# Attention values of two key heads as stacked high and low parts: 16 products for 24 per unit, halves added by a DMA that accumulates

## The reference, cut to what matters

```python
q, k, v = split(x @ w_qkv.T + b_qkv)          # 32 query heads, 8 key/value heads of 32
q = apply_rope(q, 0); k = apply_rope(k, 0)
k = jnp.repeat(k, GROUP, axis=1); v = jnp.repeat(v, GROUP, axis=1)      # GROUP = 4
scores = jnp.einsum('bhqd,bhkd->bhqk', q, k) / math.sqrt(HEAD_DIM)
attn = jax.nn.softmax(jnp.where(causal, scores, -1e20), axis=-1)
out = jnp.einsum('bhqk,bhkd->bhqd', attn, v)                            # the products that change
```

## Time and profile before

| | |
|---|---|
| median of 3 runs | 1154.16 us (1153.38 to 1154.23) |
| the profiled execution | 1153.42 us, its span 1151.3 us |
| matmuls | 6176 |
| busy: PE, PEld, DVE, ACT, POOL | 98%, 86%, 59%, 36%, 18% of the span |
| granted TensorE clock | 0.998 of full speed |
| DMA | 98.3 MB, 26% of 16 engines' time |
| chain that ended last | PE 87%, DVE 7%, ACT 4%, DMA 1% |

### The profile page before, as it was taken

One profiled execution on the slowest core, in us unless ns is written; L12 is line 12 of the kernel. 1 busy time (PEld: TensorE's weight loads), 2 busy tenths in 40 slices (PEclk: granted clock), 3 DMA queues, 4 the chain that ended last, 5 costly groups with the idle time before them and its releaser, 6 DMA issues.

```text
span 1151.3 us, 16982 instructions
## 1 busy us (share of the span) xinstructions
PE 1132.6 (98%) x6176; PEld 992.3 (86%) x6176; DVE 684.9 (59%) x1201; ACT 409.2 (36%) x1172; POOL 202.8 (18%) x131
## 2 busy tenths in 40 slices
PE   8999999999999999999989999999999999999998
PEld 6888888999999999999889998888888888888887
DVE  5312137878887888888894234233136766666664
ACT  5312124555555555555553234111123322222221
POOL 0000124443334433334351001000000000000000
PEclk9999999999999999999999999999999999999999
DMA  8020032111111111110042115473561323332222
GB/s 287 18 66 19 10 113 73 46 46 52 58 46 46 46 54 46 46 46 36 19 169 92 57 38 165 128 217 101 158 183 43 123 110 110 111 110 96 75 69 92
DMA packets 90082, 98.29 MB, mean 85 GB/s; under 512 B 7730, under 2 KB 74162, under 8 KB 90034
## 3 DMA queue, kind: packets, MB, share of 16 engines
q1 hardware_dynamic: 89890, 97.37, 26.2%
q10 hardware_dynamic: 144, 0.26, 0.1%
HBM read 72.45 MB, written 25.17 MB: 85 GB/s over the span
## 4 chain that ended last, share of the span: by engine, by line
PE 87%; DVE 7%; ACT 4%; DMA 1%; issue 0%; POOL 0%; DVEq 0%; SPq 0%
PE psum L912 18%; PE psum L1563 15%; PE psum L1871 14%; PE psum L280 13%; PE psum L1291 8%; PE psum L1851 4%; PE psum L974 4%; PE psum L1949 4%; ACT prob L617 3%; PE psum L944 3%; PE psum L959 2%; PE psum L931 1%; PE psum L991 1%; DVE prob L838 1%; DVE smax L836 1%; DVE prob L834 1%
## 5 line engine op out<-in xcount | busy, mean ns | idle before, releaser
L912 PE MATMUL psum<-p_h,c_high_low 128*128 128x512 f32 (+1 forms) x768 | 194.3, 360 | 0.5 <-DVE qkv L867 0.5
L912 PEld LDWEIGHTS psum<-p_h,c_high_low 128*128 128x128 f32 x768 | 133.2, 188 | 14.2 <-issue 0.7
L280 PE MATMUL psum<-c_high_low,w_h 128*128 128x512 f32 x384 | 119.5, 396 | 5.7 <-ACT c_high_low L215 5.7
L1563 PE MATMUL psum<-ring,rows 128*128 128x512 f32 x528 | 123.7, 392 | 1.0 <-DVE t_plain L1265 0.8
L1563 PEld LDWEIGHTS psum<-ring,rows 128*128 128x128 f32 x528 | 98.8, 188 | 23.9 <-DVE t_plain L1265 2.3
L1291 PE MATMUL psum<-chunk,rows 128*128 128x384 f32 (+1 forms) x576 | 108.7, 343 | 1.2 <-DVE qkv L867 0.7
L912 PE MATMUL psum<-p_l,c_high_low 128*128 128x512 f32 (+1 forms) x384 | 104.2, 366 | 0.0
L1291 PEld LDWEIGHTS psum<-chunk,rows 128*128 128x128 f32 x576 | 101.8, 190 | 2.0 <-DVE qkv L867 1.0
L280 PEld LDWEIGHTS psum<-c_high_low,w_h 128*128 128x128 f32 x384 | 73.4, 191 | 22.4 <-ACT c_high_low L215 5.7
L704 POOL TENSOR_TENSOR prob<-prob,sinv 128x1024 f32<-128x1024 f32 x32 | 61.1, 1908 | 126.7 <-DVE sinv L771 126.7
L694 POOL TENSOR_TENSOR c_high_low<-ring_plain,c_high_low 128x512 fp32r<-128x512 f32 x32 | 41.4, 1293 | 235.0 <-PE psum L280 139.1
(11 more groups left out here) (172 smaller groups left out, 2225.1 us busy)
## 6 DMA issues: line engine op xcount, KB each, us to landing
ring_plain<-in_x_t SPq DMA_DIRECT2D x32, 256.0 KB, 2.6
attn_scratch<-ring_plain SPq DMA_DIRECT2D x16, 512.0 KB, 2.6
ring_plain<-attn_scratch SPq DMA_DIRECT2D x32, 256.0 KB, 4.0
raw<-x_t_scratch SPq DMA_DIRECT2D x16, 512.0 KB, 4.1
rest<-in_b_base SPq DMA_DIRECT2D x16, 512.0 KB, 4.2
out<-rest SPq DMA_DIRECT2D x15, 512.0 KB, 2.7
ring_plain<-in_wqkv_t SPq DMA_DIRECT2D x10, 512.0 KB, 6.1
a_raw<-in_lora_a SPq DMA_DIRECT2D x32, 128.0 KB, 2.1
```

What stands on the lines that cost most here:

```text
L280: mm = pe.matmul(to, stationary, moving, start=k == 0 and m == 0, stop=k == KT - 1 and last, skip_group_check=True)
L912: mm = pe.matmul(to, sx[:, kk, :], moving(w, n, kk), start=first, stop=False, skip_group_check=True)
L1563: mm = pe.matmul(self.psum[:, self.BANK_OF[i], :], w[:, cols], s, start=m == 0 and p == 0, stop=m == KT - 1 and p == 2, skip_group_check=True)
```

## The change

Values: one block `vb[:, b, q, j]` holds high part and low part side by side, each with the two head columns of the pair: 2 parts x 2 heads x 32 = 128 columns. One matmul with the high probabilities gives the high product in PSUM rows 0 to 63 and the low one in rows 64 to 127. A second matmul with the low probabilities uses only the high part, 64 columns, and accumulates into rows 0 to 63. Pairs j now have PSUM columns of their own, so one b fills both banks, and b=1 waits until b=0 has been copied out (`pv_out`). Per unit 16 matmuls stand where 24 stood. ACT copies each b out in two pieces (j = 0, 1), into `ring` slot 2 and a new tile `values_odd`. When b=1 is out, POOL issues two DMAs that add rows 64 to 127 to rows 0 to 63 in SBUF, and SP stores two halves instead of one whole. In `BESIDE` the entries from `attend` b=1 on stand one pass later. Behind step 16 the loads of `b2_up` and of the first half of chunk 1 are issued ahead of the last store. The diff, without declarations:

```diff
-    def diag(vb, b, h):
+    def diag(part, b, h):
 
-        flat = vb[h * SEQ:(h + 1) * SEQ, b, :, :, :, :].rearrange("p q j c d -> p q (j c d)")
-        return flat.rearrange("p q (m d) -> p q m d", d=HD)[:, :, h:h + 7:6, :]
+        return vb[h * SEQ:(h + 1) * SEQ, b, :, :, part, h, :]
...
+            if value and not score:
+                sp.wait_ge(s_done, 2 * UNITS)
+                fold2.load_lora(sp)
+                sp.wait_ge(fold2.row_low, fold2.STAGED)
+                fold2.load_chunk(sp, 1, 0)
             if value:
-                sp.wait_ge(pv_out, 2 * w + 2)
-                sp.dma_start(a["attn"][bass.ds(w, 1), :, :].rearrange("o p c -> (o p) c"),
-                             attn[:, :, :, :].rearrange("p k b t -> p (k b t)")).then_inc(stored, 16)
+                sp.wait_ge(pv_summed, 32 * w + 32)
+                for j in range(2):
+                    sp.dma_start(a["attn"][bass.ds(w, 1), j * SEQ:(j + 1) * SEQ, :].rearrange("o p c -> (o p) c"),
+                                 values[j][high_rows, :]).then_inc(stored, 16)
...
         def values_out(w, b):
             act.wait_ge(pv_done, 2 * w + b + 1)
             if b == 0:
-                need(act, stored, 16 * w)
-            act.activation(attn[:, :, b, :], s_ps[:, b, :].rearrange("p (k t) -> p k t", k=KT), ACT.Copy).then_inc(pv_out, 1)
+                need(act, stored, 32 * w)
+            for j in range(2):
+                to = values[j].rearrange("p (k b t) -> p k b t", k=KT, b=BPU)[:, :, b, :].rearrange("p (q g) t -> p q g t", q=QUADS)
+                cols = s_ps[:, :, j * GRP * SEQ:(j + 1) * GRP * SEQ].rearrange("p q (g t) -> p q g t", g=GRP)
+                last = act.activation(to, cols, ACT.Copy)
+            last.then_inc(pv_out, 1)
...
+        def add_low_values():
+            for j in range(2):
+                pool.dma_start(values[j][high_rows, :], values[j][low_rows, :], accum_op=ALU.add).then_inc(pv_summed, 16)
...
+            if value:
+                pool.wait_ge(pv_out, 2 * w + 2)
             if nxt:
                 split_x(u + 1, 0)
...
+            if value:
+                add_low_values()
             if score:
                 normalise(v, 0)
...
-            n = 0
-            for vv, pp in ((vb_h, pt_h), (vb_l, pt_h), (vb_h, pt_l)):
+            else:
+                pe.wait_ge(pv_out, 2 * v + 1)
+            for parts, pp in ((2, pt_h), (1, pt_l)):
...
-                        mm = pe.matmul(s_ps[:, b, q * 4 * SEQ:(q + 1) * 4 * SEQ], vv[:, b, q, j, :, :].rearrange("p c d -> p (c d)"),
-                                       pp[:, q, j, :, :].rearrange("p g t -> p (g t)"), start=n == 0, stop=pp is pt_l and j == 1, skip_group_check=True)
+                        v_at = vb[:, b, q, j, 0:parts, :, :].rearrange("p m h d -> p (m h d)")
+                        mm = pe.matmul(s_ps[0:parts * SEQ, q, j * GRP * SEQ:(j + 1) * GRP * SEQ], v_at, pp[:, q, j, :, :].rearrange("p g t -> p (g t)"),
+                                       start=parts == 2 and j == 0, stop=parts == 1 and j == 1, skip_group_check=True)
...
-                  (2, 1): [(attend, 2, 1), (transpose_qk, 1, (0, 1))], (3, 1): [(transpose_qk, 1, (2,))],
-                  (4, 0): [(scores, 1, 0)], (5, 0): [(scores, 1, 1)]}
+                  (2, 2): [(attend, 2, 1), (transpose_qk, 1, (0, 1))], (3, 2): [(transpose_qk, 1, (2,))],
+                  (4, 1): [(scores, 1, 0)], (5, 1): [(scores, 1, 1)]}
```

More of the change, by code:

```diff
@@ L465, in attention @@
     v_hl = sb("v_hl", [P, 2, QUADS, 2, 2, HD], F32R)
-    vb_h, vb_l = (sb(n, [P, BPU, QUADS, 2, 4, HD], F32R) for n in ("vb_h", "vb_l"))
+    vb = sb("vb", [P, BPU, QUADS, 2, 2, 2, HD], F32R)
+    values = ring[:, 2, :], sb("values_odd", [P, D])
     prob = sb("prob", [P, BPU, 2, KVH, SEQ])
@@ L469, in attention @@
     pt_h, pt_l = (sb(n, [P, QUADS, 2, 2, P], F32R) for n in ("pt_h", "pt_l"))
-    attn = ring[:, 2, :].rearrange("p (k b t) -> p k b t", k=KT, b=BPU)
     cos, sin = sb("cos", [P, HD // 2]), sb("sin", [P, HD // 2])
@@ L497, in attention @@
     pt_done, pt_high, pt_low = sem("pt_done"), sem("pt_high"), sem("pt_low")
-    pv_done, pv_out, stored = sem("pv_done"), sem("pv_out"), sem("attn_stored")
+    pv_done, pv_out, pv_summed, stored = sem("pv_done"), sem("pv_out"), sem("pv_summed"), sem("attn_stored")
     consts = [(b_bc[:, :], a["b_qkv"].partition_broadcast(P)), (cos[:, :], a["cos"]), (sin[:, :], a["sin"]),
@@ L576, in sync @@
         steps(sp, step)
-        sp.wait_ge(stored, 16 * UNITS)
+        sp.wait_ge(stored, 32 * UNITS)
     def high_x(act, u, half):
@@ L657, in step @@
                 act.wait_ge(v_high, v + 1)
-                act.wait_ge(vb_zero, 2)
+                act.wait_ge(vb_zero, 1)
                 need(act, pv_done, 2 * v)
@@ L661, in step @@
                     for h in range(2):
-                        last = act.activation(diag(vb_h, b, h), v_hl[b * SEQ:(b + 1) * SEQ, 0, :, :, h, :].bitcast(F32), ACT.Copy)
+                        last = act.activation(diag(0, b, h), v_hl[b * SEQ:(b + 1) * SEQ, 0, :, :, h, :].bitcast(F32), ACT.Copy)
                 last.then_inc(vb_high, 1)
@@ L734, in gpsimd @@
         pool.wait_ge(fold1.done, fold1.TILES * fold1.STEPS)
-        pool.memset(vb_h[:, :, :, :, :, :].bitcast(F32), 0.0).then_inc(vb_zero, 1)
-        pool.memset(vb_l[:, :, :, :, :, :].bitcast(F32), 0.0).then_inc(vb_zero, 1)
+        pool.memset(vb[:, :, :, :, :, :, :].bitcast(F32), 0.0).then_inc(vb_zero, 1)
         steps(pool, step)
@@ L821, in step @@
                 dve.wait_ge(v_low, v + 1)
-                dve.wait_ge(vb_zero, 2)
+                dve.wait_ge(vb_zero, 1)
                 need(dve, pv_done, 2 * v)
@@ L825, in step @@
                     for h in range(2):
-                        last = dve.tensor_copy(diag(vb_l, b, h), v_hl[b * SEQ:(b + 1) * SEQ, 1, :, :, h, :].bitcast(F32))
+                        last = dve.tensor_copy(diag(1, b, h), v_hl[b * SEQ:(b + 1) * SEQ, 1, :, :, h, :].bitcast(F32))
                 last.then_inc(vb_low, 1)
@@ L1342, in sync @@
     def sync(sp):
[L1343 to L1346, removed]
+        fold.load_chunk(sp, 1, 1)
+        for s in range(2, fold.STEPS):
             for h in range(2):
-                if s > 1:
-                    sp.wait_ge(fold.chunk_low, KT * (s - 1) + HALF * (h + 1))
+                sp.wait_ge(fold.chunk_low, KT * (s - 1) + HALF * (h + 1))
                 fold.load_chunk(sp, s, h)
```

4 lines of the change are left out of this document (2 added, 2 removed).

## The result

| | before | after |
|---|---|---|
| median of 6 runs | 1153.99 us (1153.16 to 1154.23) | 1159.22 us (1157.71 to 1160.25) |
| profiled execution, span | 1151.3 us | 1158.4 us (its own time 1160.25) |
| loop's period, `up` to `up`, mean of 14 steps | 27.27 us | 27.60 us |

The ratio is 1.0045, 95% interval 1.0035 to 1.0055: slower by a half per cent, as forecast, with 128 matmuls fewer. The 14 steps of the loop take 381.8 us before and 386.4 after, which gives 4.6 of the 5.2 us between the medians.

The account below looks back on a forecast made before the run. A loop through PE, DVE and ACT, as long as PE's own work (27.25 us), was taken as the bound. Products gain 0, the second copy costs 0.40 us a step; 14 x 0.40 = +5.6 us gives 1159.4 us, range 1150 to 1166.

Parts of the forecast that it names:

- Products and moved pass: PE, attend b=1: 0.94 us saved goes to the moved pass (0.74) and a 0.2 us wait for low probabilities; gain 0.
- Second copy: ACT: keys queue behind two copies of b=1, so they and everything behind them on ACT and DVE move 0.49 us.
- Scores +0.30 and a waiting start of +0.10: PE: scores start 0.30 us later, their waiting first matmul takes 0.10 more; together +0.40 us a step.
- From scores to `up`, 10.29: DVE's chain from scores b=0 to `up`: fixed 10.29 us, holding no instruction of the change.
- PE waits ahead of `up` by 0.9 us or so: Sign: PE waits for the low LoRA rows ahead of `up` by 0.9 us or so in each step.
- PE's busy time falls by some 15 us: Sign on PE: busy time falls by some 15 us while the span grows.
- POOL and the store: POOL's two DMA issues fit its 7.41 us idle; accumulation and store have 14 us; nothing expected on the path.
- A: Rival, ACT ahead of keys: second copy fits the 0.19 us slack, period stays 27.25, time 1153 to 1156; chance 0.17.
- B: Rival: PE alone is the bound, so the 15.0 us come out in full, 1139; chance 0.11.
- C: Rival: POOL's DMAs stretch DVE's L838 by 1.40 us a step, or accumulation and store run late; 1179; chance 0.10.
- The ends: Steps 16 and 17: the copy's 0.49 us loss set against attend's 0.47 to 0.94 gain; 0, give or take 0.5.
- DVE works without a break: DVE from `up` to low probabilities b=1: continuous work ending 339.48, which nothing in the change makes earlier.

Follow-up runs that it names:

- Run 1: Kernel before plus one more ACT copy of 512 elements a row from PSUM right ahead of the keys, nothing else: 1159.28 us, ratio 1.0049.
- run 4: Changed kernel with both copies of b=1 on DVE, behind the low probabilities, instead of on ACT: 1155.13 us, ratio 1.0010.
- run 2: Kernel before without the products of low values and high probabilities, so 16 products for 24: 1154.78 us, ratio 1.0007.
- run 3: Changed kernel with the BESIDE table of before, so no pass stands later: 1158.62 us, ratio 1.0043.
- run 5: Changed kernel without the two accumulating DMAs, the store waiting for the copies alone: 1157.79 us, ratio 1.0038.
- run 12: Kernel before with one exchange on DVE, low probabilities of b=1 ahead of the low values: 1152.28 us, ratio 0.9990.
- run 8: Kernel before, DVE reordered: LoRA copy and low LoRA rows early, low probabilities b=1 ahead of low values; 24 products: 1157.48 us, ratio 1.0033.
- run 6: Changed kernel with DVE's LoRA copy ahead of b=0's reciprocal and low LoRA rows ahead of b=1's sum: 1159.4 us, ratio 1.0049.
- run 10: Changed kernel, b=1's copies on DVE, lows and low probabilities earlier, rotation sums split between POOL (after all four products) and DVE: 1144.12 us, ratio 0.9920.

## Why the prediction was right

The time was forecast at 1159.4 us and measured at 1159.22; the path was the forecast's too. That the two agree to 0.2 us is luck: the loop lost 4.6 us where the sum has 5.6, and the rest of the 5.2 lies outside the loop, where the sum has 0 and the executions scatter by 2 us with the clock. That the change costs some 5 us, and why, isn't luck: runs 1 and 4 show it from both sides.

- *Products and moved pass, gain 0.* Right. The transposes stand at 10.56 us from `up`, 10.59 before; the wait said to be 0.2 us is 0.24. Runs 2 and 3 show each half of it by itself.
- *Second copy, +0.49 on the keys.* Right: keys 0.98 us after the first copy. From the transposes to the keys it was 0.69 and is 1.17.
- *Scores +0.30 and a waiting start of +0.10.* The scores came 0.29 later against the transposes (5.02 for 4.73), the start cost 0.09. With the 0.03 by which the transposes came earlier, that is 0.35 at DVE's mask and 0.36 at the next `up` of this step, and 0.33 in the mean of the 14 steps, where 0.40 was said; the before step that was read, 27.25 us, is 0.02 under the mean of its kind. Run 1 has it without the rest of the change, run 4 takes it away.
- *From scores to `up`, 10.29.* 10.30, and the subtraction, L838 before and L856 now, at 1.22 us.
- *PE waits ahead of `up` by 0.9 us or so.* The amount is right, the place mostly wrong. By start times PE lost 0.57 us more than before ahead of L1004 and 0.17 more ahead of `up`, together the 0.74 of the moved pass. The text didn't name the wait at L1004, where the transpose of the LoRA rows waits for DVE's copy of them. It costs nothing, since `up` waits for the same engine behind it.
- *PE's busy time falls by some 15 us.* Wrong: by 5.4 us. In runs 2 and 3 it fell by 13.0 and 11.9. The likeliest reading, which no run tested by itself, is that busy time counts a matmul to its modelled end: a group of four has 0.47 us of pitch and 0.63 of busy time, so that the first 0.16 us of a wait look busy. After has three or four short waits a step, run 2 has a long one and run 3 a long and a short one. The clock has a part too: run 5, with after's order on PE and 1.000 throughout, has 1123.9 us, 3.3 less than after. PEld's busy time fell from 992.3 to 977.8, by 14.5 us. The Trainium skill's page "Perfetto Trace Analysis" (Identifying the Most-Contended Engine) says that how close TensorE is to its limit is to be read from the busy share of weight loads (and from the share of peak work), not from that of matmuls. The profiles of before and after agree in so far as 14.5 is near the 15.0 us of products and 5.4 is not; but half of the products' loads became shorter as well (137 ns for 188), so the nearness is in part chance. The forecast should have named this measure.
- *POOL and the store.* Right. SP issued the store at 328.48, 5.3 us after the issue of the second addition, and POOL kept 5.88 us of room. The estimate by the Trainium skill's page "DMA: Bandwidth & Descriptors" (Anatomy of one DMA), 2.6 us for 256 KB, was low: 3.5 and 5.1 us here.
- *The rivals.* A needed the copy to fit into 0.19 us; it took 0.48. B fell with run 2, C with run 5.
- *The ends*, 0 give or take 0.5: not resolved. The loop gives 4.6 of 5.2 us, and the remaining 0.6 is less than what the clock behind the loop moves (2 us between executions of after). The forecast had no term for the clock.

What the prediction lacked is the third member of its own loop. It treated `up` to the low probabilities as fixed, "DVE works without a break", and didn't ask what in that stretch was dear. The 2.22 us row, which served only as a price for rival C, was the place at which the kernel could be made faster.

## What to carry to other kernels

An engine that is busy for 98% can still be paced by a loop through the others: lay one step of each engine side by side, and compare what an operand's producer leaves as slack with what the change takes away. Before taking work from an engine, see whether its place in the loop waits for something, and count what the change puts ahead of the next handoff on the other engines; one copy of 0.49 us cost 0.33 us a step, and 0.94 us of matmuls gave nothing. And where several pieces tie, take them together: against the kernel before, the low probabilities first gave 1.5 us (run 12) and the two orders of DVE cost 3.8 (run 8), in the changed kernel the lows first gave nothing (run 6), and all of them with the 16 products, the copies on DVE and the split gave 0.8% (run 10).

## What the hardware showed that I had not expected

- A DVE operation on 128x640 with two operands in SBUF took 0.82 us alone. Beside an operation of POOL that had started before it, it ended 0.68 us behind POOL's end, however long that was: it took 2.22 us beside the first rotation sum in before (POOL ends at 337.33, DVE at 338.01), 1.53 us in run 6 (336.15 and 336.83), 1.31 us in run 10 (334.26 and 334.94). POOL's first rotation sum started while DVE's product before it was still running, and took 2.11 us in before where the one in run 10, beside the low probabilities, took 1.60. The low probabilities, with one operand in PSUM, took 1.21 to 1.23 us in all places. The Trainium skill's page "SBUF — State Buffer" (SBUF: two separate sides) says that of a DVE operation with two SBUF inputs and a GpSimd operation that reads SBUF the one that starts first holds the shared port for its whole instruction, and the other is blocked until then. These rows agree with that. What it did not prepare me for is how little moves such a pair together: in run 6, with no work changed, POOL's normalising ends 1.10 us later behind `up` (5.15 for 4.05) and DVE's first product, which starts 4.30 us behind `up` (4.09 in after), takes 0.71 us longer in each step.
- The accumulating DMAs within SBUF took 0.84 and 1.12 us of POOL to issue, and 3.5 and 5.1 us to land at 256 KB, where the plain store of the same size landed in 2.9 to 3.5.
- Loading the 64 columns of weights for the second matmul took 137 ns in the mean, the 128 columns for the first 188, while the product behind them has the same pitch (0.1175 us for 256 columns). The columns are not the only thing that counts: the 128 columns ahead of the transposes of probabilities (L977) took 142 ns. Rows of after:

```profile
L994 PEld LDWEIGHTS psum<-pt_h,vb 128*128 128x128 f32 x128 | 18.3, 188 | 0.4 <-ACT pt_h L620 0.4
L994 PEld LDWEIGHTS psum<-pt_l,vb 128*64 128x64 f32 x128 | 14.9, 137 | 7.3 <-DVE pt_l L767 7.3
L977 PEld LDWEIGHTS psum<-ident,prob 128*128 128x128 f32 x256 | 29.1, 142 | 2.8 <-POOL prob L715 2.8
```
